# Local attention of a sixteen-head transformer layer: another order of the softmax and the scaling on ACT and DVE, and one rotary operation on POOL

## The reference, cut to what matters

```python
q, k = l2norm(q) * qs, l2norm(k) * ksc
q = q * cos * scale + rotate_half(q) * sin * scale
k = k * cos * inv + rotate_half(k) * sin * inv
sim = einsum('bhwie,bhwje->bhwij', bq, bk2) * 8.0     # own window and the one before
attn = softmax(where(mask, -max, sim))
out = einsum('bhwij,bhwje->bhwie', attn, bv2) @ Wo     # added to x
```

## Time and profile before

| what | value |
|---|---|
| runs, median of 3 | 5413.22 us (5384.35 to 5419.07) |
| the profiled execution, its own time | 5386.55 us |
| its span, first to last instruction | 5384.8 us |
| mean granted TensorE clock | 0.900 |
| PE / PEld / DVE / ACT / POOL busy | 4535.6 / 2696.3 / 3041.0 / 2904.6 / 1985.9 us |
| first and last start of a query/key projection (L2010) | 1264.8 and 3359.4 us |

### The profile page before, as it was taken

The page is one execution under the profiler, slowest core; times in us unless marked ns, Lnnn a source line. Parts: engine busy times, 40 slices in busy tenths (PEclk is TensorE's granted clock), DMA queues, the critical chain, the costliest instruction groups (busy, mean ns, idle before and its releaser), DMA issues. The chain is left out here.

```text
span 5384.8 us, 98536 instructions
## 1 busy us (share of the span) xinstructions
PE 4535.6 (84%) x35524; PEld 2696.3 (50%) x35524; DVE 3041.0 (56%) x5774; ACT 2904.6 (54%) x8810; POOL 1985.9 (37%) x2126
## 2 busy tenths in 40 slices
PE   6998699997998979979889889855658988888999
PEld 2663355564654645646646556424445653223343
DVE  6551354455756747647557567359984554653333
ACT  4543334455756747747657577467764442553322
POOL 1320000236948939849569398013321310000000
PEclk8999789899999989999999999866669997996689
DMA  1000000001111111111111111100000000001000
GB/s 56 2 1 4 17 12 5 18 2 28 47 40 41 45 39 45 44 39 47 46 33 47 40 44 43 43 0 1 1 1 11 2 4 7 9 5 34 4 0 8
DMA packets 34474, 122.85 MB, mean 23 GB/s; under 512 B 8484, under 2 KB 9512, under 8 KB 32296
## 3 DMA queue, kind: packets, MB, share of 16 engines
q1 hardware_dynamic: 33960, 116.23, 8.0%
HBM read 37.24 MB, written 1.05 MB: 7 GB/s over the span
## 5 line engine op out<-in xcount | busy, mean ns | idle before, releaser
L706 POOL MEMSET norm_eps<- 128x1 f32 x16 | 1.6, 98 | 1596.4 <-POOLq L116 1551.9
L2149 POOL TENSOR_TENSOR local_other<-local_raw,local_sin 128x256 f32<-128x256 f32 x768 | 557.6, 726 | 60.2
L2010 PE MATMUL ps<-arena,local_xs 128*128 128x512 f32 x768 | 437.5, 654 | 111.2 <-DVE local_raw L2190 61.1
L2146 POOL TENSOR_TENSOR local_rot<-local_raw,local_cos 128x512 f32<-128x512 f32 x384 | 488.2, 1271 | 67.9 <-DVE local_raw L2190 67.9
L2152 POOL TENSOR_TENSOR local_rot<-local_rot,local_other 128x512 f32<-128x512 f32 x384 | 486.7, 1268 | 30.1
L2123 ACT ACTIVATE ps<-ps,local_negmax 128x96 f32<-128x96 f32 x1536 | 474.2, 309 | 41.5 <-DVE local_negmax L2184 41.4
L2190 DVE SCALAR_TENSOR_TENSOR local_raw<-local_inverse,ps 128x512 f32<-128x512 f32 x384 | 264.0, 687 | 278.3 <-ACT local_inverse L2117 278.3
L2180 DVE TENSOR_REDUCE local_norm<-local_squares 128x8 f32<-128x512 f32 x384 | 263.0, 685 | 129.5 <-ACT local_squares L2092 129.5
L2092 ACT ACTIVATE local_squares<-ps 128x512 f32<-128x512 f32 x384 | 229.8, 598 | 155.2 <-PE ps L2010 155.0
L2123 ACT ACTIVATION_READ_ACCUMULATOR ps<-ps,local_negmax 128x1 f32 x1536 | 309.8, 202 | 0.0
L2055 PE MATMUL ps<-const,local_probs 128*96 128x128 f32 x1536 | 239.7, 279 | 77.3 <-DVE local_probs L2208 77.3
(11 more groups left out here) (519 smaller groups left out, 10843.7 us busy)
## 6 DMA issues: line engine op xcount, KB each, us to landing
local_V_span<-local_V SPq DMA_DIRECT2D x96, 384.0 KB, 4.0
local_V_span<-local_V SPq DMA_DIRECT2D x96, 256.0 KB, 3.6
arena<-in_L1f_a SPq DMA_DIRECT2D x7, 2176.0 KB, 8.5
local_V_span<-local_V SPq DMA_DIRECT2D x72, 128.0 KB, 2.3
arena<-in_L3f SPq DMA_DIRECT2D x1, 3460.0 KB, 11.2
arena<-in_L1f_f SPq DMA_DIRECT2D x6, 537.5 KB, 3.9
arena<-in_L0f SPq DMA_DIRECT2D x1, 2824.5 KB, 9.7
arena<-in_L0x SPq DMA_DIRECT2D x1, 2049.5 KB, 9.3
```

The lines of the kernel that those rows point to most:

```text
L2010: nc.tensor.matmul(bank("qk", n)[:, :], tokens_of(tile), w("Wqkv", QKV[i] * 512, (QKV[i] + 1) * 512), start=True, stop=True)\
L2146: link(nc.gpsimd.tensor_tensor(rot, raw, m.cos[:, t, a * DH:(a + 1) * DH].unsqueeze(1) .broadcast_to([P, 8, DH]), ALU.mult))
L2149: link(nc.gpsimd.tensor_tensor(other[:, :, lo:lo + HALF], raw[:, :, HALF - lo:DH - lo], m.sin[:, t, a * DH + lo:a * DH + lo + HALF].unsque ...
```

## The change

On ACT the four exponentials of item s come ahead of the logarithm and inverse root of item n. On DVE the maxima of item s come ahead of the sums of squares of item n, and the scaling of item n goes to the end of the step, behind V copy, reciprocals and probabilities. On POOL the two operations that multiply the swapped halves with the sines become one over 512 elements, which reads `raw` with the order of the two halves reversed. No semaphore, buffer or other engine's order is changed.

```diff
--- before.py
+++ after.py
@@ -1960,6 +1960,9 @@
     def heads(a):
         return a.rearrange("p (h d) -> p h d", d=DH)
 
+    def halves(a):
+        return a.rearrange("p (h j f) -> p h j f", j=2, f=HALF)
+
     with core.stage() as st:
         xs_low, xs_high = st.sem("xs_low"), st.sem("xs_high")
         scores_ready, max_ready, exp_ready, probs_ready = (
@@ -2106,6 +2109,13 @@
                             act.wait_ge(scores_ready, 2 * (tile - 2))
                         nc.scalar.copy(m.K[:, c:c + 4, WINDOW + t * TILE:WINDOW + (t + 1) * TILE],
                                        TURN[:, :].rearrange("p (c q) -> p c q", c=4)).then_inc(flip_read, 1)
+                if 0 <= s < G:
+                    act.wait_ge(max_ready, s + 1)
+                    for u in range(UNITS):
+                        scores = SC[s % 3][:, u * SPAN:(u + 1) * SPAN]
+                        nc.scalar.activation(scores, scores, ACT.Exp, bias=m.negmax[:, s % 2, u:u + 1],
+                                             accum_out=m.total[:, s % 2, u:u + 1])\
+                          .then_inc(exp_ready, 1)
                 n = s + LEAD
                 if n < G:
                     act.wait_ge(summed, n + 1)
@@ -2116,13 +2126,6 @@
                     act.wait_ge(log_ready, n + 1)
                     nc.scalar.activation(m.inverse[:, n % 4, :], m.log[:, n % 4, :], ACT.Exp, scale=-0.5)\
                       .then_inc(inverted, 1)
-                if 0 <= s < G:
-                    act.wait_ge(max_ready, s + 1)
-                    for u in range(UNITS):
-                        scores = SC[s % 3][:, u * SPAN:(u + 1) * SPAN]
-                        nc.scalar.activation(scores, scores, ACT.Exp, bias=m.negmax[:, s % 2, u:u + 1],
-                                             accum_out=m.total[:, s % 2, u:u + 1])\
-                          .then_inc(exp_ready, 1)
                 g = s - 1
                 if 0 <= g < G:
                     act.wait_ge(turned, g + 1)
@@ -2145,10 +2148,9 @@
                     pool.wait_ge(flipped, n - 3)
                 link(nc.gpsimd.tensor_tensor(rot, raw, m.cos[:, t, a * DH:(a + 1) * DH].unsqueeze(1)
                                              .broadcast_to([P, 8, DH]), ALU.mult))
-                for lo in (0, HALF):
-                    link(nc.gpsimd.tensor_tensor(other[:, :, lo:lo + HALF], raw[:, :, HALF - lo:DH - lo],
-                                                 m.sin[:, t, a * DH + lo:a * DH + lo + HALF].unsqueeze(1)
-                                                 .broadcast_to([P, 8, HALF]), ALU.mult))
+                link(nc.gpsimd.tensor_tensor(halves(m.other[:, :]), halves(m.raw[:, n % 4, :])[:, :, ::-1, :],
+                                             m.sin[:, t, a * DH:(a + 1) * DH].rearrange("p (j f) -> p j f", f=HALF)
+                                             .unsqueeze(1).broadcast_to([P, 8, 2, HALF]), ALU.mult))
                 nc.gpsimd.tensor_tensor(rot, rot, other, ALU.add).then_inc(rotated, 1)
 
         @st.block.vector
@@ -2172,6 +2174,10 @@
                     dve.wait_ge(projected, tile + 1)
                     nc.vector.tensor_tensor(place_x, bank("out", tile)[:, 0:TILE], place_x, ALU.add)\
                       .then_inc(x_done, 1)
+                if 0 <= s < G:
+                    dve.wait_ge(scores_ready, s // 2 + 1)
+                    nc.vector.tensor_reduce(m.negmax[:, s % 2, :], sc, AX_X, ALU.max, negate=True)\
+                      .then_inc(max_ready, 1)
                 n = s + LEAD
                 if n < G:
                     dve.wait_ge(squared, n + 1)
@@ -2179,18 +2185,6 @@
                         dve.wait_ge(inverted, n - 3)
                     nc.vector.tensor_reduce(m.norm[:, n % 4, :], heads(m.squares[:, n % 2, :]), AX_X, ALU.add)\
                       .then_inc(summed, 1)
-                if 0 <= s < G:
-                    dve.wait_ge(scores_ready, s // 2 + 1)
-                    nc.vector.tensor_reduce(m.negmax[:, s % 2, :], sc, AX_X, ALU.max, negate=True)\
-                      .then_inc(max_ready, 1)
-                if n < G:
-                    if n >= 4:
-                        dve.wait_ge(rotated, n - 3)
-                    dve.wait_ge(inverted, n + 1)
-                    nc.vector.scalar_tensor_tensor(out=heads(m.raw[:, n % 4, :]),
-                                                   in0=m.inverse[:, n % 4, :].unsqueeze(2).broadcast_to([P, 8, DH]),
-                                                   scalar=1e12, in1=heads(bank("qk", n)[:, :]), op0=ALU.min, op1=ALU.mult)\
-                      .then_inc(scaled, 1)
                 if values_at(s) is not None:
                     tile, i = values_at(s)
                     v = 2 * tile + i
@@ -2207,6 +2201,14 @@
                         dve.wait_ge(turned, s - 1)
                     nc.vector.tensor_tensor(m.probs[:, s % 2, :, :], sc, m.total[:, s % 2, :].unsqueeze(2)
                                             .broadcast_to([P, UNITS, SPAN]), ALU.mult).then_inc(probs_ready, 1)
+                if n < G:
+                    if n >= 4:
+                        dve.wait_ge(rotated, n - 3)
+                    dve.wait_ge(inverted, n + 1)
+                    nc.vector.scalar_tensor_tensor(out=heads(m.raw[:, n % 4, :]),
+                                                   in0=m.inverse[:, n % 4, :].unsqueeze(2).broadcast_to([P, 8, DH]),
+                                                   scalar=1e12, in1=heads(bank("qk", n)[:, :]), op0=ALU.min, op1=ALU.mult)\
+                      .then_inc(scaled, 1)
 
 
 def gelu_ffn(core, arena, m):
```

## The result

The changed kernel takes 5650.91 us (median of 4 runs, 5645.99 to 5652.5); the kernel before 5398.78 us (median of 4 runs, the three shown ahead among them, 5378.83 to 5419.07). The ratio is 1.0467, 95% interval 1.0438 to 1.0497: slower by 4.7%.

A forecast was written before the change was run, and what follows sets the result against it. Projections wait for DVE's scaling through two shared PSUM banks, and exponentials now lie inside that chain: +3.06 us a pattern, +41.7 us a call, +250 us over six calls on 5386.55, say 5640 us; range 5560 to 5720.

The forecast's parts named there:

- the six calls: The local attention's six calls, the only code the change touches; forecast to take 250 us more in all.
- qk: PE's projection of queries or keys in a step; its PSUM bank is shared in turn with V and Wo products.
- POOL at 90%: Rival, mid-call: POOL was the bound, so lighter POOL work brings PE's own 16.63 us a pattern, 5296 us; chance 0.06.
- the wait in step 2: Before the change, PE idles 0.42 us ahead of this step's qk, waiting for DVE's scaled rows.
- the hand-off of 0.06 us in step 1: Before the change, scaling ends at 1416.64 and this step's qk starts at 1416.70: no slack.
- pattern: Four successive steps, numbered s mod 4 from 0, in a local attention call; forecast to go from 17.71 to 20.77 us.
- The three legs: Times between qk starts: step 0 to 1, 6.24 us; 1 to 2, 4.99; 2 through 3 to next 0, 9.54.
- The merged operation: POOL's rotary halves in one 512-element operation: 1.27 us taken, saving 0.26 us a step, without effect on the time.
- The sum: 14 patterns a call at 20.77 us make 290.8 us, +41.7 a call, +250 us over six calls.
- The heads of the calls: Start of each call, no exponentials yet, set by POOL: gains 1 us, given back by the first step's flip wait.
- The wait of step 0: PE's wait for the scaling at this step's qk; such waits were forecast at 0.7 to 1.6 us each.
- that rival: The clock falls as PE idles more, adding 3.5 to 5.5 us a pattern: 5930 us and above; chance 0.05.

## Why the prediction was right

- *The time.* 5640 us was forecast; 5650.91 was measured, 5645.99 in the profiled execution. The mechanism and its size are right, but part of the closeness is luck: the six calls cost 243.7 us and not 250, and the code behind the last qk took 17 us longer in this execution than in the profiled one of before, which no term of the sum holds.
- *What bounds it.* That POOL at 90% was not the bound, while projections waited for the scaling, was read from the wait in step 2 and the hand-off of 0.06 us in step 1. The run with the merge alone shows it: POOL relieved, pattern unchanged. The Trainium skill's rule to relieve the engine of the highest occupancy first ("Perfetto Trace Analysis", Identifying the Most-Contended Engine) would have pointed at POOL; this case doesn't bear it out (17.70 us a pattern with POOL relieved).
- *The three legs.* Worked out as 6.24, 4.99 and 9.54 us, measured 6.23, 4.99 and 9.54. They held because all durations and hand-offs stood in the rows; only their order was new. (The 1.41 us from the first exponential to the reciprocal, which stand in all three, are 1.42 to 1.44 in the changed kernel's pattern.) The runs that free one bank after another shorten the leg that belongs to it.
- *The merged operation.* Taken at 1.27 us, measured 1.271. The estimate from the Trainium skill's price for small reads ("GPSIMD Engine Reference", Performance pitfalls for Q7 kernels), 1.4 us more, is not borne out: the reversed halves cost nothing that shows.
- *The sum.* +250 us forecast; +243.7 from the first qk to the last. 14 patterns were worked out at 290.8 us; in the six calls they take 289.0 to 293.2 us, together 252.7 more than before. The heads of the calls, up to qk of s = 0, take 4.8 us less (1 us a call was forecast), and the stretches between the calls 4.4 less. The other 15.7 us of the difference between the spans lie outside.
- *Small misses.* The wait of step 0 was given as at least 0.7 us and is 0.50, partly because the transposes for the probabilities start at 5.83 after qk2, not at 5.76, and partly because idle time in the rows counts from the modelled end of the Wo product. The clock stays full in the middle of a call, as forecast; but the price of that rival was real, as the run with the scaling alone last shows, and what was held against it, the full clock at the start of a call, did not last: in the same window of the changed kernel, 1284 to 1296 us, the granted clock is 0.72, with PE busy for 9.32 of 12 us.
- *Where my expectations of the experiments failed.* One mistake came back with the Wo product in a score bank, with all products there, and with the copy moved ahead: a bank that is free when a product is written must also be read in time for its next user, and that reader, the addition to x, stands behind DVE's last work of step 3, which is the scaling in the new order and the probabilities in the old. Two more were off by the clock (the scaling alone last) and by PE's own work (queries and keys alone in the two banks).

## What to carry to other kernels

Ask of every instruction that frees a buffer what stands ahead of it on its engine, and who waits for the buffer; an instruction that looks like bookkeeping (here a scaling, last reader of a PSUM bank) can be the one that paces the loop. Where a reordering costs more than it should, don't judge the order before the buffers: the same order was the worse or the better one according to how many uses lay between a bank's writer and its next. And add up the durations along one whole pattern, leg by leg, before trusting the busiest engine.

## What was not expected of the hardware

The clock of a later stage, whose code is the same in all kernels, differs between executions by as much as several of these effects are worth. Windows of the last layer's cross attention, first in the changed kernel, then in the kernel with only the order changed (columns as in the earlier trace rows):

```profile
5230.00:5330.00 100.00, 96.49 (x488) 41.87 (x490) 35.44 (x78) 32.35 (x62) 0.00 (x0) 0.50 0.02 5
```

```profile
5240.00:5340.00 100.00, 85.38 (x642) 37.37 (x642) 40.82 (x99) 46.42 (x88) 0.00 (x0) 0.89 0.02 5
```

The granted clock there was 0.50 in the one, half speed, and 0.89 in the other, and from the last qk to the end of the span it took 2042.4 us (5644.2 - 3601.8) and 1981.1 us (5595.3 - 3614.2). Over the fourteen traces of this document that remainder takes 1978 to 1983 us in three, 2025 in three (that of the kernel before is one) and 2042 to 2049 in eight: three levels, and not a spread. What decides it was not tried. It is why kernels here are compared by their patterns, and why one time alone can differ by some 60 us without any cause in the edit.
